# Booking the mask of the diagonal to VectorE in the order of a causal attention layer

## The reference, cut to what matters

```python
x = x + _L0_attn_ref(_layernorm(x), w_qkv, w_proj, b_proj)
x = x + _L0_ffn_ref(_layernorm(x), theta, phi, theta_noise, phi_noise)
# attention: 16 heads of 16 features
Q, K = apply_rope(Q), apply_rope(K)
attn = einsum('bqhd,bkhd->bhqk', Q, K) * scale
attn = where(causal, attn, -1e9)          # a query sees keys up to its own place
attn = softmax(attn)
out = einsum('bhqk,bkhd->bqhd', attn, V) @ w_proj + b_proj
# feed-forward
real, imag = x @ cos(theta + theta_noise), x @ sin(phi + phi_noise)
return sqrt(real * real + imag * imag)
```

## Time and profile before

| | before |
|---|---|
| median of 3 runs | 2035.52 us (2033.64 to 2036.34) |
| the profiled execution | 2035.29 us |
| its span, from the first to the last instruction | 2033.5 us |
| mean granted TensorE clock | 0.995 of full speed |
| busy: TensorE, VectorE, ScalarE, GpSimd | 98%, 74%, 68%, 42% |

### The profile page before, as it was taken

One profiled execution on the slowest core, in us unless ns is written; L12 is line 12 of the kernel. 1 busy time (PEld: TensorE's weight loads), 2 busy tenths in 40 slices (PEclk: granted clock), 3 DMA queues, 4 the chain that ended last, 5 costly groups with the idle time before them and its releaser, 6 DMA issues.

```text
span 2033.5 us, 38813 instructions
## 1 busy us (share of the span) xinstructions
PE 1998.3 (98%) x13028; PEld 856.6 (42%) x13028; DVE 1508.7 (74%) x2757; ACT 1390.4 (68%) x2687; POOL 857.9 (42%) x1335
## 2 busy tenths in 40 slices
PE   7999999999999999999999999999999999999998
PEld 4343443344443444444444443444444344433334
DVE  5888787887778677786767868688677867667835
ACT  3367677776667676777667676687766767667774
POOL 3622425363443435543363442546434363351132
PEclk9999999999999999999999999999999999999999
DMA  6310222231111221221122111222111222130122
GB/s 140 74 43 17 69 61 70 62 84 55 57 60 55 68 70 58 75 87 61 60 65 73 63 55 53 80 87 73 58 54 60 70 70 79 29 117 6 48 89 68
DMA packets 130761, 133.35 MB, mean 66 GB/s; under 512 B 29435, under 2 KB 105723, under 8 KB 130555
## 3 DMA queue, kind: packets, MB, share of 16 engines
q1 hardware_dynamic: 127728, 128.29, 20.5%
q10 hardware_dynamic: 2832, 2.56, 0.7%
HBM read 38.49 MB, written 25.68 MB: 32 GB/s over the span
## 4 chain that ended last, share of the span: by engine, by line
PE 87%; POOL 3%; issue 2%; ACT 2%; DVE 2%; SPq 2%; DMA 1%; DVEq 0%; POOLq 0%; ACTq 0%
PE banks L1049 22%; PE banks L1064 22%; PE banks L1027 21%; PE banks L971 5%; PE banks L982 5%; PE banks L1025 3%; PE banks L1009 3%; PE banks L916 3%; DVE chunk_max L1361 2%; ACT probs L1168 1%; SPq L731 1%; PE banks L905 1%; PE banks L898 1%; POOL guess L664 1%; ACT inverse L1188 1%
## 5 line engine op out<-in xcount | busy, mean ns | idle before, releaser
L1361 DVE TENSOR_REDUCE chunk_max<-banks 128x1 f32<-128x512 f32 (+3 forms) x2240 | 1351.8, 667 | 404.8 <-PE banks L1027 401.9
L1168 ACT ACTIVATE probs<-banks 128x512 f32<-128x512 f32 (+1 forms) x2240 | 1139.2, 602 | 356.0 <-PE banks L1049 274.7
L1027 PE MATMUL banks<-stack_k,stack_q 96*128 96x512 bf16 (+3 forms) x2560 | 730.0, 349 | 1.8 <-DVE chunk_max L1361 0.7
L1049 PE MATMUL banks<-stack_q,stack_k 99*128 99x512 bf16 (+3 forms) x2560 | 694.6, 349 | 4.4 <-ACT probs L1168 2.2
L1064 PE MATMUL banks<-probs,v_one 128*17 128x512 f32 (+3 forms) x5120 | 528.5, 532 | 3.6 <-POOL probs L1488 2.8
L1049 PEld LDWEIGHTS banks<-stack_q,stack_k 99*128 99x128 bf16 x2560 | 229.3, 97 | 375.1 <-ACT probs L1168 182.2
L1027 PEld LDWEIGHTS banks<-stack_k,stack_q 96*128 96x128 bf16 x2560 | 240.3, 98 | 244.8 <-DVE chunk_max L1361 71.4
L1488 POOL TENSOR_SCALAR_AFFINE_SELECT probs<-probs 128x512 f32<-128x512 f32 x256 | 162.7, 644 | 350.9 <-ACT probs L1168 348.8
L1064 PEld LDWEIGHTS banks<-probs,v_one 128*17 128x17 f32 x5120 | 118.6, 96 | 280.3 <-issue 175.1
L1025 PE MATMUL banks<-diag_mask,ident_bf 128*128 128x128 bf16 x1024 | 199.2, 221 | 5.1 <-DVE chunk_max L1361 4.2
L1472 POOL TENSOR_SCALAR max_neg<-row_max 128x16 f32<-128x16 f32 x64 | 16.3, 255 | 313.5 <-DVE row_max L1370 239.4
(11 more groups left out here) (156 smaller groups left out, 1146.3 us busy)
## 6 DMA issues: line engine op xcount, KB each, us to landing
stack_q<-parts SPq DMA_DIRECT2D x384, 64.0 KB, 2.6
stack_k<-parts SPq DMA_DIRECT2D x354, 64.0 KB, 2.6
sums<-o_raw SPq DMA_DIRECT2D x64, 256.0 KB, 2.3
rot<-raw SPq DMA_DIRECT2D x236, 64.0 KB, 2.0
xin<-x SPq DMA_DIRECT2D x16, 512.0 KB, 4.1
heads_t<-sums SPq DMA_DIRECT2D x26, 256.0 KB
mid<-x SPq DMA_DIRECT2D x13, 512.0 KB, 4.1
inverse<-inverses SPq DMA_DIRECT2D x26, 256.0 KB
```

The lines of the kernel that those rows point to most:

```text
L1027: mm = nc.tensor.matmul(bank[:, n * wide:(n + 1) * wide], stack_q[u % 2][0:SPLIT_ROWS, t, h + n, j * P:(j + 1) * P], stack_k[u % 2][0:SPLI ...
L1049: mm = nc.tensor.matmul(bank[:, a * wide:(a + 1) * wide], stack_k[u % 2][0:ROWS, j // SUB, first + a, (j % SUB) * P:(j % SUB + 1) * P], st ...
L1168: nc.scalar.activation(probs[:, g % PROBS, first:first + many, w0:SPAN], bank, ACT.Exp).then_inc(s_exp, 1)
L1361: nc.vector.tensor_reduce(to, bank[:, 0:count * wide].rearrange("p (h n) -> p h n", h=count), AX.X, ALU.max).then_inc(s_emptied["DVE"], 1)
```

## The change

Only `plan()`'s bookings change, beside a constant and a helper. `masks(n)` says whether a bank with n heads is masked by VectorE; with `MASKED_HEADS = 4` it is true for every bank. For a bank on the diagonal the booking on TensorE loses 0.06 us a head, and the booking on VectorE becomes 0.13 us a head plus the width, where it was 0.07 us a bank plus the width. `maximum_scores` and `reduce_out`, which issue the instructions, are not in the diff, and `LOWEST` is used nowhere.

```diff
+LOWEST = -3e38
...
+def masks(count):
+
+    return count <= MASKED_HEADS
...
+MASKED_HEADS = 4
...
-                job(name, "PE", 0.01 + wide / 2400 + (0.06 * n if d == tile // SUB else 0.0), at + step * done / total - MAX_FIRST,
+                job(name, "PE", 0.01 + wide / 2400 + (0.06 * n if d == tile // SUB and not masks(n) else 0.0), at + step * done / total - MAX_FIRST,
                     [before_max, *((f, u, k) for f in ("fetch", "fetch_k") for k in range(c + 1)), begun(at + step * done / total - MAX_SLACK)])
-                with_bank(name, name, "DVE", 0.07 + wide / 970, at + step * done / total)
+                with_bank(name, name, "DVE", (0.13 if d == tile // SUB and masks(n) else 0.07 / n) * n + wide / 970, at + step * done / total)
```

## The result

| | before | changed kernel |
|---|---|---|
| median | 2035.93 us (4 runs, 2033.64 to 2036.66) | 2055.68 us (4 runs, 2054.31 to 2056.0) |
| profiled span, clock | 2033.5 us, 0.995 | 2053.6 us, 0.993 |

The ratio is 1.0097, with a 95% interval of 1.0081 to 1.0113: 19.75 us slower. I had said 2045, so the direction was right and the size, 9.8 us over before, half of what came. 2055.7 lies just above the forecast's own range (2040 to 2055) and inside the wide one (to 2058).

The account below looks back on a forecast made before the run. TensorE's streamed list was taken as the bound. From 2035.3 us, +13.5 for passes, +0.5 idle matmuls, -5 for the wait at 1791 us and +1 other waits gave 2045 us; own range 2040 to 2055, 8 in 10 2034 to 2058.

Parts of the forecast that it names:

- What bounds the kernel: Whole kernel: time is TensorE's list streaming through, busy 1998.3 of 2033.5 us; more VectorE work costs nothing unless concentrated.
- That the change issues no mask on VectorE: Diagonal banks: only bookings move; TensorE's list keeps 1024 masks and VectorE's reductions stay the same.
- Passes, +13.5 us: TensorE's list, throughout: 58 more passes of the values at 0.2325 us each for leaving and re-entering bf16 matmuls.
- Idle matmuls, +0.5: Start of TensorE's list: four more idle matmuls at 0.23 us, between 0 and 0.9 us lost, 0.5 taken.
- the start, at most 3 either way: Start, with 16.7 idle us on TensorE: the changed order could give or take about 3 us.
- The wait at 1791 us, -5 us: Denominator inversion near the end: TensorE's 3.40 us wait shrinks to about 1.4, saving 2.0 of wait and 2.9 of clock.
- Other waits, +1 us: All remaining waits, start included: more room for VectorE and an order made for other durations oppose; +1 us taken.
- A: Rival: filled-bank waits vanish from 150 us on and offset the passes, so the kernel is not slower; chance 0.13.
- D: Rival: the passes' cost is hidden where TensorE would have waited otherwise, 2035 to 2039 us; chance 0.05.
- B: Rival: the order fits the chip worse, new waits of 3.4 us plus 2.9 of clock come up, 2062 us; chance 0.12.
- C: Rival: TensorE really loses 1024 masks, 61 us less, 1974 us; no chance worth a number.

Follow-up runs that it names:

- e7: Changed kernel with the mask really on VectorE in all diagonal banks, joined with the maximum per head, none on TensorE: 2020.82 us, ratio 0.9936.
- e1: Kernel before, TensorE's list cut at 70 places by moving a filling of maxima ahead of a values pass's last step: 2050.58 us, ratio 1.0075.
- e2: As e1, plus preceding fillings of maxima moved behind a pass's first step, 134 more passes than the kernel before: 2060.72 us, ratio 1.0127.
- e10: Kernel before with only VectorE's booking changed, to 0.13 us a head on the diagonal, TensorE's booking as before: 2050.26 us, ratio 1.0075.
- e13: Changed kernel with SyncE's load of the twelfth block's denominators moved ahead of the last unit's twelve slot transfers: 2056.47 us, ratio 1.011.
- e5: Kernel before with the change's bookings for the first unit alone, all other units as before: 2036.66 us, ratio 1.001.

## Why the prediction was right in sign and half in size

- **What bounds the kernel: right, with one sentence too wide.** Every order of the same work that has more passes was slower than before, if not in proportion. But I had written that more work on VectorE would cost nothing unless it fell into one place. In e7 VectorE's busy time is 51 us longer than in the changed kernel, spread over the program, and 26 of the 61 us that TensorE was spared didn't come off the time.
- **That the change issues no mask on VectorE: right.** 1024 masks and 2240 reductions stand in both profiles.
- **Passes, +13.5 us: right, a little high.** The cut lists give 58 x 0.19 to 0.22 = 11 to 13 us, the medians 12.6. The middle, with 48 of the 58 passes, shows 11.0 us, 0.23 each. By the trace the time of all passes above their steps went from 76.8 to 92.8 us, 16 us: 12.6 for 58 passes and 3.4 for waits inside them.
- **Idle matmuls, +0.5, and the start, at most 3 either way: too small.** The profile has 4.1 us, 0.9 of them the idle matmuls, and the isolated start 2.5 us. I had put the start among the other waits, with both signs open.
- **The wait at 1791 us, -5 us: the step that failed.** It failed twice. I let the load follow the copy of the maximum by 3.3 us, as I counted what stands between the rows and the load and not the twelve slot transfers ahead of the rows, which I had only as a bound. It followed by 9.2 us, and as the inversion moved up by 7 us and the landing of the load by 4, TensorE's wait grew to 5.04 us where I had it shrink to 1.4. And the wait was worth nothing to begin with: four experiments that moved or removed it left the time as it was, as the slots of the last unit (changed kernel) or GpSimd's load (before) end the same stretch. So taking it away would have gained 0 and not 5 us. With 0 the sum is 2050.3 us.
- **Other waits, +1 us: too small.** In the profiles 20.1 us were lost: 12.6 by passes, 0.9 by idle matmuls, and 6.6 by waits and the lower clock, where I had -4 for both wait terms together. Of the 6.6, 3.2 came up at the start, 0.6 in the middle and 2.8 behind step 545. The visible waits there are the place itself (1.6 us more), the filling behind it (1.4) and the last values (0.9), 3.9 together, so about 1 us of hidden waits seems to have gone. These sizes are read after the fact from one profile of each kernel; only the start has an experiment of its own, and what makes its waits longer I did not follow.
- **Rivals.** A and D fall with e1 and e2. A trace of A may be there: TensorE's busy time grew by 10.5 us, and passes and idle matmuls make 13.5, so some hidden waits seem to have gone. B, more places with waits, holds in part: none of its 6.3 us places came up in the middle, but the end is worse. C was the right thing to rule out, and e7 shows that the step it names would have been the gain, though 35 us of its 61.

## What to carry to other kernels

A wait that stands in the profile with its length is worth that length only if nothing behind it is late too: before it enters a sum, look for the next semaphore that the same engine needs from another chain, and whether that one has slack. Count transitions between kinds of work in an in-order list, and price them from many blocks of different length; but don't expect fewer transitions to pay, if the blocks then wait inside. A lag between two orders, read at one step, holds the work that has moved across it: take that out first. A planner's booking that the instructions don't match can cost time even where it errs toward leaving room, as the booking on VectorE alone did here (e10, 15 us).

## What the runs showed of the hardware

- One change from bf16 matmuls on the whole array to float32 matmuls in four column groups and back costs 0.22 us together (medians of 82, 73, 42 and 13 passes of one to four steps in the kernel before), while a change to float32 matmuls on the whole array and back costs nothing that shows (1.71 us for four instructions of 0.429).
- Four float32 matmuls of 17 stationary and 512 moving columns, one in each column group, take 0.858 us together, as much as one float32 matmul of 512 columns on the whole array (two instructions of 0.429).
- On VectorE a reduction that masks (`tensor_tensor_reduce`) takes 700 ns for 512 columns, where the plain one takes 683, but each is followed by a read of the accumulator of 140 ns (e7).
- Behind the first 100 us, every wait of TensorE of 2.8 us or more in these profiles went with a stretch at a granted clock of 0.5, the level of 1.2 GHz. It began before the wait was over or about 1 us later at most: 1804.7 to 1811.6 us in the changed kernel, whose wait ended at 1807.62, and 1838.5 to 1845.3 us in e13, whose wait ended at 1840.66. Its length is not fixed by the list: at the place of rows 7 it was 6.8 us in the kernel before, after a wait of 3.40 us, and 3.4 us in e5, after a wait of 2.93, a difference of 1.7 us at full clock. The changed kernel also has such a stretch, 1350.8 to 1354.2 us, where no wait was longer than 0.6 us.
